# A four-layer transformer stack on one core: the experts' down projection with routed activations stationary

## The chip, the core and the metric

One core of one Trainium2 chip runs the whole program. The metric is the device time of one execution in microseconds (us). Engines are named as the profile names them: PE (TensorE matmul; PEld its weight loads), DVE (VectorE), ACT (ScalarE), POOL (GpSimd), SP (SyncE, which issues DMAs).

## What is computed

32 sequences of 256 tokens with 128 features run through four sublayers, each with a residual and a layer norm:

```python
x = ln(x + linear_attention(x))          # stage a
x = ln(x + low_rank_expert_ffn(x))       # stage b
x = ln(x + causal_softmax_attention(x))  # stage c
x = ln(x + moe(x))                       # stages r (router), d (experts), e (last norm)
```

The change lies in the last one. 16 experts of 64 hidden units are computed for every token, weighted by a grouped top-4 router, and a shared expert of 128 units is added:

```python
g = silu(einsum('th,efh->tef', x, w1_e)); u = einsum('th,efh->tef', x, w3_e)
routed = einsum('tef,ehf,te->th', g * u, w2_e, combine)
out = routed + (silu(x @ w1_s.T) * (x @ w3_s.T)) @ w2_s.T
```

## The kernel before

The tokens are cut into 16 blocks of 512 (four tiles of 128 tokens). The kernel is a software pipeline whose order is written out by hand, engine by engine: `turn(i)` issues stage a of block i, stage b and the start of c of block i-1, the rest of c and the router r of block i-2, the experts d of block i-3, and the last norm e of block i-4. There are 20 turns: six written out (LEAD), a loop of five passes with two turns each, four written out to drain. Engines wait for one another by semaphores with a counter per step; each engine runs its own list in order.

The experts' 16 x 64 hidden units and the shared expert's 128 are nine chunks of 128 units (ALLCH = 9). For chunk c, PE's `d_hidden` makes the gate (bank GB) and the up product (bank UB), three products of 512 columns each (L351 to L353; weights are split into a high and a low part). ACT's `d_silu` (L738) makes silu of GB, DVE's `d_gu` (L1067) multiplies by UB, and DVE's `d_hid` (L1077) by the router's weights, which lie transposed in bank CB; chunk 8, the shared expert, needs no weights and goes straight to hid (L1070). hid has 128 units on the partitions and 512 tokens along the free axis, two buffers. Then PE's `d_down` (L548) multiplies by the down weights w2: w2 is the stationary operand (128 x 128), hid streams through with 512 columns, and nine such products add up in bank YB. So YB holds y transposed: features on the partitions, tokens along. ACT's `d_y` (L740, at the end of the turn) copies YB to SBUF as yT, and PE's `d_yT` (L558) transposes its four tiles back into YB in the next turn, between the scores of stage c (`c_scores`) and the v product of stage a (`a_vT_`). DVE's `d_res` (L1079) adds the residual x3 and takes the norm's statistics.

Other steps that the prediction names: `a_vT_` waits for x0T_lo, which POOL makes (L1196) from ACT's copies of the transposed input; `c_av` (L510 to L512) multiplies the attention's probabilities, copied by ACT (L709, probT), with the values; `b_up` (L466, L467) waits for ACT's copy downT (L690); L454, L483 and L523 are other products whose stationary operand is an activation tile of 128 tokens. The small step L360 is the transpose of four tiles. At the program's end only e of the last block remains.

Of the kernel before, what the change touches and what calls it, by code (L numbers as in the profile page):

```python
# [26 lines left out]
ACT = mybir.ActivationFunctionType  # L27
# [5 lines left out]
P = 128  # L33
SEQ = 256
TILES = 4
BLOCK = TILES * P
# [7 lines left out]
CHUNKS = EXPERTS * EF // P  # L44
# [3 lines left out]
ALLCH = CHUNKS + 1  # L48
# [58 lines left out]
def started(n):  # L107

    return not (isinstance(n, int) and n == 0)


def build(nc, x_dram, weight_dram, whole_dram, out_dram):
# [13 lines left out]
    with ExitStack() as ctx:  # L126
        def sb(name, shape, dt=F32):
            return ctx.enter_context(nc.sbuf_tensor(name, shape, dt))

        def sig(name, per=1):  # L130
            return Signal(ctx.enter_context(nc.semaphore(name)), per)
# [3 lines left out]
        GB, UB, CB, YB = bank[0:4]  # L135
# [7 lines left out]
        whole = sb("whole", [P, N_CONST])  # L143
# [21 lines left out]
        def const(name, parts=P):  # L165
            a, b = CONST_COLS[name]
            return whole[0:parts, a:b]

        ident = const("ident")
# [99 lines left out]
        silu = sb("silu", [P, 2, BLOCK])  # L269
        gu = sb("gu", [P, 2, BLOCK])  # L270
        hid = sb("hid", [P, 2, BLOCK])
        yT = sb("yT", [P, BLOCK])


        w_in, k_in, late_in, x_st = sig("w_in"), sig("k_in"), sig("late_in"), sig("x_st", 16)
# [24 lines left out]
                                                        sig("a_exp", 4), sig("a_pT", 2), sig("v_rinv"))  # L300
        R_MASKED, R_TOP = 13, 17
        p_gate, a_ez, v_r, p_cT = sig("p_gate"), sig("a_ez"), sig("v_r", 29), sig("p_cT")
        p_G, p_U, p_w2, p_yT = sig("p_G", ALLCH), sig("p_U", ALLCH), sig("p_w2", ALLCH), sig("p_yT")
        a_silu, v_gu, v_hid, a_y = sig("a_silu", ALLCH), sig("v_gu", ALLCH), sig("v_hid", CHUNKS), sig("a_y")

        block = ctx.enter_context(nc.Block())

# [38 lines left out]
        def _(pe):  # L346
            mm = nc.tensor.matmul
# [7 lines left out]
            def tile(ap, t):  # L355
                return ap[:, t * P:(t + 1) * P]

            def transpose_tiles(out, src, eye, parts=P):
                for t in range(TILES):
                    last = nc.tensor.transpose(out[0:parts, t * P:(t + 1) * P], src(t), eye)  # L360
                return last
# [186 lines left out]
            def d_down(n, c):  # L548
                if c < CHUNKS:
                    pe.wait_ge(v_hid.sem, v_hid.at(n, c + 1))  # L550
                else:
                    pe.wait_ge(v_gu.sem, v_gu.at(n))
                if c == 0 and started(n):
                    pe.wait_ge(v_res[3].sem, v_res[3].at(n - 1))
                a = CONST_COLS["w2"][0] + c * P
                mm(YB[:], whole[:, a:a + P], hid[:, c % 2], start=c == 0, stop=c == CHUNKS).then_inc(p_w2.sem, 1)  # L556

            def d_yT(n):  # L558
                pe.wait_ge(a_y.sem, a_y.at(n))
                transpose_tiles(YB, lambda t: tile(yT, t), ident).then_inc(p_yT.sem, 1)  # L560

            def turn(i, odd, load=None):
                a, b, c, d, e = live(i), live(i - 1), live(i - 2), live(i - 3), live(i - 4)
                if a: a_xT_(i, odd, load)
                if d: d_hidden(i - 3, 1 - odd, 0)
                if d: d_cT(i - 3)
                if c: c_scores(i - 2)
                if e: d_yT(i - 4)
                if a: a_vT_(i)
                if d: d_hidden(i - 3, 1 - odd, 1)  # L570
                if c: c_pT(i - 2)
                if a: a_qk(i)
                if c: c_av(i - 2)
                if b: b_xT(i - 1)
                if a: a_g_(i)
                if d: d_down(i - 3, 0)
                if b: b_small(i - 1)
                if a: a_v_(i)
                if d: d_hidden(i - 3, 1 - odd, 2)
                if a: a_kv(i)  # L580
                if a: a_qT_(i)
                if d: d_hidden(i - 3, 1 - odd, 3)
                if d: d_down(i - 3, 1)
                if d: d_hidden(i - 3, 1 - odd, 4)
                if a: a_num_(i)
                if d: d_down(i - 3, 2)
                if c: r_xT(i - 2, odd)
                if d: d_down(i - 3, 3)
                if d: d_hidden(i - 3, 1 - odd, 5)
                if c: r_gate(i - 2)  # L590
                if b: b_dnT(i - 1)
                if d: d_down(i - 3, 4)
                if b: b_up(i - 1)
                if d: d_hidden(i - 3, 1 - odd, 6)
                if d: d_down(i - 3, 5)
                if a: a_aT(i)
                if d: d_hidden(i - 3, 1 - odd, 7)
                if d: d_down(i - 3, 6)
                if d: d_hidden(i - 3, 1 - odd, 8)
                if b: c_xT(i - 1)  # L600
                if a: a_out(i)
                if d: d_down(i - 3, 7)
                if b: c_project(i - 1)
                if d: d_down(i - 3, 8)
                if b: c_value(i - 1)
# [11 lines left out]
        def _(act):  # L617
            fn = nc.scalar.activation
# [118 lines left out]
                    act.wait_ge(v_gu.sem, v_gu.at(n, max(c - 1, 0)))  # L737
                fn(silu[:, c % 2], GB[:], ACT.Silu).then_inc(a_silu.sem, 1)  # L738

            def d_y(n):  # L740
                act.wait_ge(p_w2.sem, p_w2.at(n))
                fn(yT[:], YB[:], ACT.Copy).then_inc(a_y.sem, 1)

            def turn(i, odd):
                a, b, c, d, e = live(i), live(i - 1), live(i - 2), live(i - 3), live(i - 4)
                if d: d_silu(i - 3, 0)
                if a: x0_hi(i)
                if second(i): split_late()
                if c: c_exp(i - 2)
                if a: a_vT_(i)  # L750
                if c: c_pT(i - 2)
                if d: d_silu(i - 3, 1)
                if b: copy_xT(i - 1, 1, B0)
                if b: b_small(i - 1)
                if a: a_g_(i)
                if a: a_v_(i)
                if a: a_tap0(i)
                if d: d_silu(i - 3, 2)
                if a: a_qT_(i)
                if d: d_silu(i - 3, 3)  # L760
                if b: b_exp(i - 1)
                if c: c_norm(i - 2, odd)
                if d: d_silu(i - 3, 4)
                if c: r_hi(i - 2, odd)
                if d: d_silu(i - 3, 5)
                if c: r_exp(i - 2)
                if b: b_dnT(i - 1)
                if d: d_silu(i - 3, 6)
                if e: e_norm(i - 4)
                if d: d_silu(i - 3, 7)  # L770
                if b: b_layer_norm(i - 1)
                if d: d_silu(i - 3, 8)
                if b: copy_xT(i - 1, 2, B0)
                if b: c_qkv(i - 1)
                if d: d_y(i - 3)

            for i in range(LEAD):
                turn(i, i % 2)
# [8 lines left out]
        def _(dve):  # L787
# [18 lines left out]
            a, b = WEIGHT_COLS["logit"]  # L806
# [4 lines left out]
            a, b = WEIGHT_COLS["base"]  # L811
# [267 lines left out]
            def d_res(n, odd):  # L1079
                if started(n):  # L1080
                    dve.wait_ge(a_x4.sem, a_x4.at(n - 1))
                dve.wait_ge(p_yT.sem, p_yT.at(n))
                tt(res[3][:], x3[odd][:], tiles(YB[:]), ALU.add).then_inc(v_res[3].sem, 1)
                norm_stats(3, n)

# [217 lines left out]
```

## Time and profile before

| | us |
|---|---|
| median of 3 runs (lowest, highest) | 725.48 (723.78, 726.61) |
| span of the profiled execution | 722.4 |
| PE busy (weight loads PEld) | 659.3 (508.6) |
| DVE, ACT, POOL busy | 587.1, 486.4, 309.0 |

The profile gives no time of its own for the profiled execution beside its span from the first to the last instruction; the runs' median lies 3.1 us above it. Busy times are unions of instructions that overlap. A matmul's recorded length includes its way through the array and is modelled, so for a stream of products the step from one start to the next is the better measure. An f32 product shows as two records with a weight load each. "idle before" in brackets is the time in which the engine did nothing, and what ended it; "issue" means that nothing which the profile shows was waited for.

### The profile page before, as it was taken

The page shows a single profiled execution, that of the slowest core. Times are in us where ns is not written, and L with a number is a line of the kernel's source. Part 1 is how long each engine was busy: PE and PEld are TensorE (multiplying, and loading weights), DVE is VectorE, ACT ScalarE, POOL GpSimd, SP SyncE. Part 2 cuts the span into 40 slices and gives each one's busy share as a digit, 9 for nine tenths or more (in the row PEclk, how much of TensorE's full clock was granted, in tenths as well). Part 3 has the DMA queues.
Part 4 walks back from the last instruction along what each step waited for, and adds up shares of the span by engine and source line. Part 5 has one row for each costly group of instructions (what it writes and reads, how often), then busy time and mean ns, then how long its engine had stood idle before and what let it go on. Part 6 is the DMA issues. An engine that isn't in the chain of part 4 may idle for free.

```text
span 722.4 us, 13085 instructions
## 1 busy us (share of the span) xinstructions
PE 659.3 (91%) x3654; PEld 508.6 (70%) x3654; DVE 587.1 (81%) x1873; ACT 486.4 (67%) x978; POOL 309.0 (43%) x793
## 2 busy tenths in 40 slices
PE   3466679999999999999999999999999999999994
PEld 2354557787878777777878787777868787767652
DVE  1566778989898898889898898889897998877672
ACT  2243548587786878686877877686877868676623
POOL 1234443445453535536454535436454535340311
PEclk9787979999999999999999999999999999999997
DMA  6000000000000010101000000101000000000001
GB/s 226 12 4 15 1 16 0 16 1 16 15 15 15 1 30 2 31 0 29 0 15 16 5 25 0 30 0 29 0 21 9 15 0 0 15 1 15 16 0 30
DMA packets 18678, 12.51 MB, mean 17 GB/s; under 512 B 704, under 2 KB 18240, under 8 KB 18368
## 3 DMA queue, kind: packets, MB, share of 16 engines
q1 hardware_dynamic: 18624, 11.95, 5.5%
q8 instruction: 15, 0.25, 0.2%
q14 instruction: 39, 0.32, 0.1%
HBM read 7.75 MB, written 4.19 MB: 17 GB/s over the span
## 4 chain that ended last, share of the span: by engine, by line
PE 68%; DVE 14%; ACT 7%; issue 6%; POOL 3%; DMA 1%; DVEq 0%; ACTq 0%; SPq 0%; POOLq 0%
PE bank L556 13%; PE bank L351 8%; PE bank L353 8%; PE bank L352 8%; PE bank L360 8%; PE bank L439 2%; PE bank L466 2%; PE bank L411 2%; PE bank L454 2%; DVE conv L954 2%; DVE gu L1067 1%; PE bank L477 1%; PE bank L510 1%; PE bank L478 1%; PE bank L523 1%
## 5 line engine op out<-in xcount | busy, mean ns | idle before, releaser
L556 PE MATMUL bank<-hid,whole 128*128 128x512 f32 x288 | 147.2, 593 | 0.8 <-DVE hid L1070 0.8
L351 PE MATMUL bank<-x3T_hi,w_hi 128*128 128x512 f32 x288 | 138.2, 480 | 1.8 <-DVE gu L1067 1.4
L738 ACT ACTIVATE silu<-bank 128x512 f32<-128x512 f32 x144 | 86.4, 600 | 65.0 <-PE bank L353 61.9
L1067 DVE TENSOR_TENSOR gu<-silu,bank 128x512 f32<-128x512 f32 x128 | 86.7, 677 | 41.1 <-ACT silu L738 18.5
L353 PE MATMUL bank<-x3T_hi,w_lo 128*128 128x512 f32 x288 | 113.5, 394 | 0.0
L352 PE MATMUL bank<-x3T_lo,w_hi 128*128 128x512 f32 x288 | 112.7, 391 | 0.0
L1171 POOL TENSOR_TENSOR moment<-stats 128x4 f32<-128x4 f32 x192 | 44.8, 266 | 150.1 <-DVE stats L881 134.3
L1077 DVE TENSOR_TENSOR hid<-gu,bank 128x512 f32<-128x512 f32 x128 | 87.2, 681 | 1.8 <-PE bank L556 0.8
L351 PEld LDWEIGHTS bank<-x3T_hi,w_hi 128*128 128x128 f32 x288 | 54.2, 188 | 31.0 <-ACT silu L738 9.9
L1157 POOL TENSOR_TENSOR qk<-rope_c,rope_s 128x512 f32<-128x512 f32 x32 | 40.6, 1280 | 82.6 <-DVE rope_s L843 82.6
L1171 POOL TENSOR_TENSOR rstd<-moment,whole 128x4 f32<-128x4 f32 x64 | 64.7, 1011 | 5.0
L352 PEld LDWEIGHTS bank<-x3T_lo,w_hi 128*128 128x128 f32 x288 | 54.5, 189 | 16.3 <-issue 10.0
L353 PEld LDWEIGHTS bank<-x3T_hi,w_lo 128*128 128x128 f32 x288 | 54.0, 188 | 12.4
L556 PEld LDWEIGHTS bank<-hid,whole 128*128 128x128 f32 x288 | 49.7, 189 | 15.3 <-issue 7.2
L1201 POOL TENSOR_TENSOR x3T_lo<-x3T,x3T_hi 128x512 fp32r<-128x512 f32 x16 | 22.0, 1375 | 87.9 <-ACT x3T_hi L728 87.9
L738 ACT ACT_TABLE_LOAD x45 | 57.7, 1283 | 0.8
L954 DVE SCALAR_TENSOR_TENSOR conv<-vT,whole,conv 128x512 f32<-128x512 f32 x64 | 54.4, 850 | 0.8
L881 DVE BATCH_NORM_STATS2 stats<-res 128x6 f32<-128x128 f32 x192 | 41.9, 281 | 1.6
L1171 POOL TENSOR_TENSOR moment<-moment,whole 128x4 f32<-128x4 f32 x192 | 35.6, 202 | 5.0
L644 ACT ACTIVATE x<-bank,shift,rstd 128x128 f32<-128x128 f32 x64 | 24.1, 457 | 19.1 <-POOL shift L1171 19.1
L360 PEld LDWEIGHTS bank<-whole,x 128*128 128x128 f32 x192 | 23.7, 144 | 18.3 <-ACT x L644 7.9
L360 PE MATMUL bank<-whole,x 128*128 128x128 f32 x192 | 30.0, 280 | 7.1 <-ACT x L644 6.8
(196 smaller groups left out, 1635.7 us busy)
## 6 DMA issues: line engine op xcount, KB each, us to landing
x_in<-x SPq DMA_DIRECT2D x16, 256.0 KB, 2.9
out<-x SPq DMA_DIRECT2D x16, 256.0 KB, 2.3
whole<-w_whole SPq DMA_DIRECT2D x1, 1198.5 KB, 5.7
w_raw<-w SPq DMA_DIRECT2D x1, 1152.0 KB
w_raw<-w SPq DMA_DIRECT2D x1, 546.0 KB, 7.0
whole<-w_whole SPq DMA_DIRECT2D x16, 32.0 KB
whole<-w_whole SPq DMA_DIRECT2D x1, 64.0 KB
```

The lines of the kernel that those rows point to most:

```text
L351: mm(out, wh, mh, start=True, stop=False)
L352: mm(out, wh, ml, start=False, stop=False)
L353: return mm(out, wl, mh, start=False, stop=True)
L360: last = nc.tensor.transpose(out[0:parts, t * P:(t + 1) * P], src(t), eye)
L556: mm(YB[:], whole[:, a:a + P], hid[:, c % 2], start=c == 0, stop=c == CHUNKS).then_inc(p_w2.sem, 1)
L738: fn(silu[:, c % 2], GB[:], ACT.Silu).then_inc(a_silu.sem, 1)
L881: nc.vector.bn_stats(stats[k][:, t, :], res[k][:, t, :]).then_inc(v_st[k].sem, 1)
L954: stt(conv[:], vT[:, :, j:j + SEQ], taps[:, j:j + 1], conv[:], ALU.mult, ALU.add).then_inc(v_conv.sem, 1)
L1067: tt(gu[:, c % 2], silu[:, c % 2], UB[:], ALU.mult).then_inc(v_gu.sem, 1)
L1077: tt(hid[:, c % 2], gu[:, c % 2], CB[:], ALU.mult).then_inc(v_hid.sem, 1)
L1157: tt(qk[:, 2 * h:2 * h + 2, :].rearrange("p t d -> p (t d)"), rope_c[:, h], rope_s[:, h], ALU.add).then_inc(g_qk.sem, 1)
L1171: tt(out, in0, in1, op).then_inc(g_ln[k].sem, 1)
```

## The change

The operands of the down projection change places. For each chunk, each tile of 128 tokens of hid becomes the stationary operand, and w2's 128 columns stream through it: four products of 128 columns instead of one of 512. Each writes its own quarter of YB, so YB now holds y itself, tokens on the partitions, after nine chunks. The copy `d_y` on ACT, the transposes `d_yT` on PE, the buffer yT and their semaphores are gone; `d_res` on DVE waits for the last down product. Chunk 0's first product alone carries the start flag of the bank, the last product of chunk 8 the stop flag.

```diff
-                mm(YB[:], whole[:, a:a + P], hid[:, c % 2], start=c == 0, stop=c == CHUNKS).then_inc(p_w2.sem, 1)
-
-            def d_yT(n):
-                pe.wait_ge(a_y.sem, a_y.at(n))
-                transpose_tiles(YB, lambda t: tile(yT, t), ident).then_inc(p_yT.sem, 1)
+
+                for t in range(TILES):
+                    last = mm(tile(YB, t), hid[:, c % 2, t * P:(t + 1) * P], whole[:, a:a + P], start=c == 0 and t == 0,
+                              stop=c == CHUNKS and t == TILES - 1, skip_group_check=True)
+                last.then_inc(p_w2.sem, 1)
...
-                if e: d_yT(i - 4)
...
-            def d_y(n):
-                act.wait_ge(p_w2.sem, p_w2.at(n))
-                fn(yT[:], YB[:], ACT.Copy).then_inc(a_y.sem, 1)
...
-                if d: d_y(i - 3)
...
             def d_res(n, odd):
                 if started(n):
                     dve.wait_ge(a_x4.sem, a_x4.at(n - 1))
-                dve.wait_ge(p_yT.sem, p_yT.at(n))
+                dve.wait_ge(p_w2.sem, p_w2.at(n))
```

PE's list at the end of the loop's second turn, before. Banks are PSUM banks, `whole` holds the constants and w2, `x2T` is stage c's input; "x3" is three more of the same.

```order
L439 MATMUL bank<-whole,oT 128x128 [waits g_oT]
L439 MATMUL bank<-whole,oT 128x128 x3
L556 MATMUL bank<-hid,whole 128x512 [waits v_hid]
L477 MATMUL bank<-x2T,w_raw 128x512 [waits a_x2T]
L478 MATMUL bank<-x2T,w_raw 128x512
L552 REGISTER_ALU
L556 MATMUL bank<-hid,whole 128x512 [waits v_gu]
L483 MATMUL bank<-w_raw,x2T 128x128 [waits a_cq]
L483 MATMUL bank<-w_raw,x2T 128x128 x3
L609 COMPARE_AND_BRANCH
```

The same place after (line numbers move by one or two).

```order
L438 MATMUL bank<-whole,oT 128x128 [waits g_oT]
L438 MATMUL bank<-whole,oT 128x128 x3
L557 MATMUL bank<-whole,hid 128x128 [waits v_hid]
L557 MATMUL bank<-whole,hid 128x128 x3
L476 MATMUL bank<-x2T,w_raw 128x512 [waits a_x2T]
L477 MATMUL bank<-x2T,w_raw 128x512
L551 REGISTER_ALU
L557 MATMUL bank<-whole,hid 128x128 [waits v_gu]
L557 MATMUL bank<-whole,hid 128x128 x3
L482 MATMUL bank<-w_raw,x2T 128x128 [waits a_cq]
L482 MATMUL bank<-w_raw,x2T 128x128 x3
L607 COMPARE_AND_BRANCH
```

Nothing moves; each down product is four, and the first of them carries the wait. At the start of the loop's first turn PE's list before reads, from the last scores of stage c on (`x0T_hi` and `x0T_lo` are the two parts of stage a's transposed input, `x3T` those of the experts'):

```order
L497 MATMUL bank<-causal_b,ident_b 128x128
L498 MATMUL bank<-ckT,cqT 128x128
L360 MATMUL bank<-whole,yT 128x128 [waits a_y]
L360 MATMUL bank<-whole,yT 128x128 x3
L385 REGISTER_ALU
L351 MATMUL bank<-x0T_hi,w_hi 128x512 [waits v_res0,g_x0l]
L352 MATMUL bank<-x0T_lo,w_hi 128x512
L353 MATMUL bank<-x0T_hi,w_lo 128x512
```

And after:

```order
L496 MATMUL bank<-causal_b,ident_b 128x128
L497 MATMUL bank<-ckT,cqT 128x128
L384 REGISTER_ALU
L350 MATMUL bank<-x0T_hi,w_hi 128x512 [waits v_res0,g_x0l]
L351 MATMUL bank<-x0T_lo,w_hi 128x512
L352 MATMUL bank<-x0T_hi,w_lo 128x512
```

The two rows on yT are gone and what stood behind them follows at once. On DVE, `d_res` in the loop's first turn before:

```order
L886 TENSOR_SCALAR x<-res,mean,rstd 128x128 x3
L1081 ISA
L1083 TENSOR_TENSOR res<-x_0,bank 128x512 [waits p_yT,a_x4]
L881 BN_STATS stats<-res 128x6 [waits v_res3]
L881 BN_STATS stats<-res 128x6 x3
```

And after:

```order
L879 TENSOR_SCALAR x<-res,mean,rstd 128x128 x3
L1074 ISA
L1075 ISA [waits a_x4]
L1076 TENSOR_TENSOR res<-x_0,bank 128x512 [waits p_w2]
L874 BN_STATS stats<-res 128x6 [waits v_res3]
L874 BN_STATS stats<-res 128x6 x3
```

The add waits for the down product, and its wait for a_x4 has become a row of its own. The lists of POOL and SP are the same.

## Rows read from the trace of the kernel before

**Rows 1.** The page: busy time of each engine, and the granted clock by slices.
```profile
PE 659.3 (91%) x3654; PEld 508.6 (70%) x3654; DVE 587.1 (81%) x1873; ACT 486.4 (67%) x978; POOL 309.0 (43%) x793
...
PEclk9787979999999999999999999999999999999997
```

**Rows 2.** Timeline of PE at a turn's end: start, length, engine, line, what, [idle before].
```profile
421.01 1.02 PE L556 MATMUL bank<-hid,whole 128*128 128x512 f32 x2
421.87 1.05 PE L483 MATMUL bank<-w_raw,x2T 128*128 128x128 f32 x8
422.76 0.60 PE L360 MATMUL bank<-whole,x_in 128*128 128x128 f32 x4
```

**Rows 3.** Timeline of ACT, POOL and PE at the start of the next turn.
```profile
424.09 0.60 ACT L738 ACTIVATE silu<-bank 128x512 f32<-128x512 f32 x1 [1.42 <-PE bank L353]
...
425.80 1.28 POOL L1196 TENSOR_TENSOR x0T_lo<-x0T,x0T_hi 128x512 fp32r<-128x512 f32 x1 [2.25 <-ACT x0T L650]
...
426.79 0.60 PE L360 MATMUL bank<-whole,yT 128*128 128x128 f32 x4
427.15 0.49 PE L351 MATMUL bank<-x0T_hi,w_hi 128*128 128x512 f32 x1
...
430.51 0.85 ACT L709 ACTIVATE probT<-bank 128x384 f32<-128x384 f32 x2
...
431.42 0.49 PE L510 MATMUL bank<-cv,probT 128*128 128x128 f32 x2
```

**Rows 4.** Timeline of PE and DVE around the loop's jump back at 380 to 386 us.
```profile
351.12 0.38 PE L510 MATMUL bank<-cv,probT 128*128 128x128 f32 x1
...
358.13 0.69 DVE L1067 TENSOR_TENSOR gu<-silu,bank 128x512 f32<-128x512 f32 x1 [1.26 <-ACT silu L738]
...
381.37 1.05 PE L483 MATMUL bank<-w_raw,x2T 128*128 128x128 f32 x8
382.26 0.60 PE L360 MATMUL bank<-whole,x_in 128*128 128x128 f32 x4
...
385.93 0.69 DVE L1067 TENSOR_TENSOR gu<-silu,bank 128x512 f32<-128x512 f32 x1 [1.79 <-issue]
...
391.62 0.49 PE L510 MATMUL bank<-cv,probT 128*128 128x128 f32 x2 [0.47 <-ACT probT L709]
391.94 0.39 PE L511 MATMUL bank<-cv,probT 128*128 128x128 f32 x2
```

**Rows 5.** Timeline around chunk 4's down product: PE and ACT.
```profile
407.19 0.96 PE L523 MATMUL bank<-w_raw,x3T 128*128 128x16 f32 x8
407.99 0.62 PE L360 MATMUL bank<-whole,down_x 128*96 128x128 f32 x4
408.45 1.02 PE L556 MATMUL bank<-hid,whole 128*128 128x512 f32 x2
...
408.70 0.58 ACT L690 ACTIVATE downT<-bank 96x512 fp32r<-96x512 f32 x1
...
409.34 0.49 PE L466 MATMUL bank<-w_raw,x1T 128*128 128x128 f32 x2
```

**Rows 6.** Timeline of PE: two forms of product before a hidden product.
```profile
622.49 1.05 PE L483 MATMUL bank<-w_raw,x2T 128*128 128x128 f32 x8
...
623.62 0.39 PE L352 MATMUL bank<-x3T_lo,w_hi 128*128 128x512 f32 x1
...
637.29 1.02 PE L556 MATMUL bank<-hid,whole 128*128 128x512 f32 x2
...
638.38 0.40 PE L352 MATMUL bank<-x3T_lo,w_hi 128*128 128x512 f32 x1
```

**Rows 7.** Timeline of the last drained turns: the transposes, and the chain at the end.
```profile
691.64 0.60 PE L360 MATMUL bank<-whole,yT 128*128 128x128 f32 x4
...
711.76 0.60 ACT L742 ACTIVATE yT<-bank 128x512 f32<-128x512 f32 x1 [2.04 <-PE bank L556]
...
713.17 0.69 DVE L1083 TENSOR_TENSOR res<-x,bank 128x512 f32<-128x512 f32 x1 [2.63 <-PE bank L360]
```

More of the change, by code:

```diff
@@ L271, in build @@
         hid = sb("hid", [P, 2, BLOCK])
-        yT = sb("yT", [P, BLOCK])
         w_in, k_in, late_in, x_st = sig("w_in"), sig("k_in"), sig("late_in"), sig("x_st", 16)
@@ L302, in build @@
         p_gate, a_ez, v_r, p_cT = sig("p_gate"), sig("a_ez"), sig("v_r", 29), sig("p_cT")
-        p_G, p_U, p_w2, p_yT = sig("p_G", ALLCH), sig("p_U", ALLCH), sig("p_w2", ALLCH), sig("p_yT")
-        a_silu, v_gu, v_hid, a_y = sig("a_silu", ALLCH), sig("v_gu", ALLCH), sig("v_hid", CHUNKS), sig("a_y")
+        p_G, p_U, p_w2 = sig("p_G", ALLCH), sig("p_U", ALLCH), sig("p_w2", ALLCH)
+        a_silu, v_gu, v_hid = sig("a_silu", ALLCH), sig("v_gu", ALLCH), sig("v_hid", CHUNKS)
         block = ctx.enter_context(nc.Block())
```

## The prediction

> **What bounds the kernel now.** I read the page first. PE is busy 91% of the span and PEclk is 9 in all but the first slices, so TensorE runs at its full clock level in the middle [rows 1]. In 40 us of timeline from the middle, PE's records follow each other with hardly a gap. The reader is to see three things there.
>
> First, what a down product costs. Its two records are recorded 1.02 us long, but ends are modelled, so I use the step from one group's start to the next: 421.01 to 421.87, 0.86 us [rows 2].
>
> Second, the short stretch at the start of a turn, from silu of chunk 0 to the attention product L510. PE is *not* alone on the path there. POOL's x0T_lo starts at 425.80 and takes 1.28, to 427.08; PE's next product that needs it (L351 on x0T_hi) starts at 427.15, right after the four yT transposes (426.79 to 427.15) [rows 3]. No row of ACT shows idle time from 424.09 (silu) to 431.36, the end of the second probT copy (430.51 + 0.85), and L510 starts at 431.42, with no idle time of PE noted before it [rows 3]. So PE, POOL and ACT arrive together, within a few hundredths of a microsecond.
>
> Third, the turn that follows the loop's jump back. DVE's gu comes 1.79 us late there with "issue" as reason, the row maxima and so ACT's exponentials are late, and PE stands idle for 0.47 us before L510 [rows 4]. Back from that gu, DVE has no other gap to 358.13, where it waited for ACT's silu of chunk 2 of the turn before [rows 4]. L510 to L510 is 431.42 - 391.62 = 39.80 us without the jump and 391.62 - 351.12 = 40.50 with it [rows 3, 4]. There are 4 jumps (5 passes of two turns).
>
> **What it removes.** Per block: four transposes on PE, one ACT copy of 0.60 us, and two hand-overs between engines. The ACT copy is worth nothing inside: ACT is idle 1.42 us right behind it, until PE has produced chunk 0's first product [rows 3]. The transposes (0.36 us from start to start) are worth nothing inside either: without them PE is done with c_scores at 426.79, but x0T_lo is there only at 427.08, as before. PE then waits about 0.3 us instead of transposing, and further on probT would hold it anyway. Value taken in a whole turn: 0; its bounds are 0 and 0.36. Only at the very end, where nothing else runs, the chain shows: ACT's copy starts at 711.76 and DVE's residual add at 713.17 [rows 7]; the add now waits for the product itself, so the end comes 713.17 - 711.76 = 1.41 us earlier. In turn 18 (a drained one) PE has just waited for comb, and the transposes at 691.64 lie between that and hidden chunk 1 [rows 7]. There up to 0.36 goes; since the next products wait for DVE's gu too, I take 0.26.
>
> **What it adds.** 144 chunks each have four products of 128 columns (eight records, eight weight loads) for one of 512 columns (two and two). The trace has the same form: L483, four f32 products of 128 columns, each with a new activation tile stationary. It takes 421.87 to 422.76, 0.89 us [rows 2]. That is 111 ns a record, against 0.43 us for 512 columns. Are the loads hidden? L523 has only 16 columns, so its eight loads set its pace: 407.19 to 407.99, 0.80 us or 100 ns a load [rows 5]. 100 is under 111, so yes. The Trainium skill, "TensorE: Matmul & The Clock Gate", section "Back-to-back issue gap", gives N/2.4 + 2.5 ns per matmul; by it six more records would cost an estimated 15 ns a chunk, and the sum below would come out near 0 and not at +1.6; the rows show more than that per short f32 record, and I go by the rows.
>
> What follows counts too. Three of a turn's nine chunks stand before a hidden product, whose first load has little to hide behind. From the down product to L352's start the old form takes 637.29 to 638.38, 1.09 us; the short form, L483 before the same product, 622.49 to 623.62, 1.13 [rows 6]. So +0.04 there, +0.03 elsewhere: I take **35 ns a chunk**. Its lower bound is 0 (the columns streamed are the same, so a gain is out); the upper one follows under the rivals.
>
> Where does it count? Chunk 4 is hidden: behind it L466 starts at 409.34, and ACT's downT ends at 408.70 + 0.58 = 409.28; the product itself, from 408.45, would be through at 408.45 + 0.86 = 409.31 [rows 5]. PE waits there by 0.03 already, so chunk 4 may grow by that at no cost. The other eight lie between L510 and the next silu of chunk 0, where PE is full: 8 x 0.035 = **+0.28 us a turn**. In the four turns with a jump, DVE holds the end of the interval, and its chain hangs on hidden chunk 2; of the eight only chunk 0 comes before that, so +0.035, and the other 0.25 vanish in the 0.47 us that PE stood waiting.
>
> DVE's add waits for p_w2 and not p_yT: it was never late for its transposes but at the end, and p_w2 comes sooner; nothing behind it on DVE changes. In one of the loop's two turns a wait becomes an instruction of its own on DVE (the order shows it): it comes after the row maxima, off the chain above, and costs nothing. POOL and SP have the same rows. PE's products and loads grow from 3654 to 3654 + 144 x 6 - 64 = 4454 each.
>
> **The sum.** The blocks end at L510 of turns 4 to 16: 9 intervals without a jump x 0.28 = +2.52; 4 with it x 0.035 = +0.14; the three drained turns +0.3 (some 16 chunks that count x 0.035 = 0.56, less 0.26); the end -1.41 + 0.035 = -1.38. With d for the price of a chunk that is 72d + 4d + 16d - 0.26 + d - 1.41 = 93d - 1.67. Together **+1.6 us**: the span goes from 722.4 to 724.0. The span lies 3.1 us below the median of the runs, 725.48; what lies around it stays, so 727.1.
>
> **The rivals.**
> A, the forecast above: 727.1.
> B, the transposes' time is real gain. If the tie at L351 and L510 is looser than I read it (another order of arrival in other turns), the nine intervals lose 0.36 each: 1.6 - 3.2 = -1.6, so 723.9; in the jump turns too, 722.4. Against it: POOL's row and PE's start fit to 0.07, and ACT has no gap.
> C, the short products are dearer. When the stream is broken, the first product takes 391.62 to 391.94, 0.32, where one of L483's takes 0.89 / 4 = 0.22 [rows 2, 4]. If each chunk pays half of that break, 0.05, on top of 0.035, then 93 x 0.085 - 1.67 = +6.2: 731.7. With the whole break it is 93 x 0.135 - 1.67 = +10.9, and the jump turns' slack is used up, so some 737; that is the upper bound. It decides from 0.057 us a chunk on, where +3.6 is reached. Against it: L483 begins with a load of an activation tile too, and its 0.89 contains it.
> D, PE's loop body grows by 200 products and loads in all (100 a turn), and PE too starts to lose time at the jump, as DVE does with 1.79 us. Now it loses none: from L483 to the x_in transposes it is 0.89 at a jump (381.37 to 382.26) and 0.89 without [rows 2, 4]. If it lost DVE's 1.79 less the 0.47 that PE stands there anyway, 4 x 1.3 = +5.3 comes on top: 732.4. The Trainium skill, "Runtime: NRT & Kernel Launch", section "Instruction fetch mechanics", says that a taken branch whose target has left the engine's instruction window forces a fetch; by that rule a longer body could lose its start, and DVE's row agrees with it; that PE's body stays inside is shown by no row for the longer one.
> E, the change doesn't do what it says: the order shows the four products and no yT row, so this is out.
>
> **How the numbers follow.** A 0.68, B 0.12, C 0.10, D 0.06, anything else 0.04. The runs lie within 0.25% of their median, and about 0.5% (3.6 us) is what a measurement can tell from no change. Faster means under 721.9: part of B and of the rest, 0.05. Slower means over 729.1: C and D but for their mild ends, and a part of the rest, 0.15. Same: 0.80. The range is B's 723 to 730.5, which leaves out most of C and D and half of the rest, together under 0.2.
>
> **What would show it.** In the profile after: chunk to next group 0.89 instead of 0.86; PE's wait for POOL's x0T_lo, hidden before, now in nearly every turn with about 0.3 us; L510 to L510 near 40.08 without a jump and 40.53 with one; no gap on ACT before probT; the end 1.4 us shorter from the last product on. A gap of PE behind the jump speaks for D, groups over 0.95 for C, and intervals under 39.8 for B. If ACT's chain from silu of chunk 0 to probT gets shorter than 431.36 - 424.09 = 7.27 us, my main step is wrong.

## The result, and the profile of the changed kernel

The changed kernel takes 726.19 us (median), the kernel before 725.07 us: a ratio of 1.0015, 95% interval 1.0009 to 1.0021. That is 1.1 us more, 0.7 to 1.5 by the interval. The forecast was +1.6 us, 727.1 us in all, with a chance of 0.80 on "same".

The page of the changed kernel: busy time, granted clock, and the shares of the chain that ended last.

```profile
PE 661.8 (91%) x4454; PEld 585.2 (81%) x4454; DVE 587.0 (81%) x1873; ACT 475.6 (66%) x962; POOL 308.2 (43%) x793
...
PEclk9778969999999999999999999999999999999997
...
PE 64%; DVE 13%; ACT 9%; issue 7%; POOL 5%; DMA 1%; DVEq 0%; ACTq 0%; SPq 0%; POOLq 0%
```

PE has its 4454 products and as many loads, and it is busy only 2.5 us longer than in [rows 1]; loads are busy 77 us longer and hardly show. The clock is the same in the long middle.

Timeline of the changed kernel, PE at a turn's end, the lines that answer to [rows 2]: one chunk's short products, then the 128-column products after it.

```profile
423.83 1.05 PE L557 MATMUL bank<-whole,hid 128*128 128x128 f32 x8
424.72 1.06 PE L482 MATMUL bank<-w_raw,x2T 128*128 128x128 f32 x8
425.61 0.60 PE L359 MATMUL bank<-whole,x_in 128*128 128x128 f32 x4
```

The chunk takes 424.72 - 423.83 = 0.89 us where it took 0.86.

Timeline of ACT, POOL and PE at the start of the next turn (answers to [rows 3]), and PE behind a jump of the loop (answers to [rows 4]).

```profile
426.95 0.60 ACT L736 ACTIVATE silu<-bank 128x512 f32<-128x512 f32 x1 [2.23 <-PE bank L352]
...
428.66 1.27 POOL L1189 TENSOR_TENSOR x0T_lo<-x0T,x0T_hi 128x512 fp32r<-128x512 f32 x1 [2.49 <-ACT x0T L648]
...
429.38 0.44 PE L497 MATMUL bank<-ckT,cqT 128*128 128x128 f32 x2
429.99 0.51 PE L350 MATMUL bank<-x0T_hi,w_hi 128*128 128x512 f32 x1 [0.17 <-POOL x0T_lo L1189]
...
433.36 0.85 ACT L707 ACTIVATE probT<-bank 128x384 f32<-128x384 f32 x2
...
434.27 0.48 PE L509 MATMUL bank<-cv,probT 128*128 128x128 f32 x2
```

```profile
394.20 0.49 PE L509 MATMUL bank<-cv,probT 128*128 128x128 f32 x2 [0.40 <-ACT probT L707]
```

The four transposes of yT are gone from between the scores (L497) and v's transposed product (L350), and in their place PE waits for POOL's x0T_lo, which ends at 428.66 + 1.27 = 429.93. The row says 0.17 of idle time, but ends of products are modelled; the whole step from L497 to L350 is 0.61 us, and a kernel shown below does it in 0.20 us when nothing is waited for. The product by probT (L509 now, L510 before) comes 434.27 - 394.20 = 40.07 us after the one before it; it was 39.80 in [rows 3, 4].

The waits of PE on POOL and ACT at these two places: in all us, times, longest.

```profile
PE bank L350 <- POOL x0T_lo L1189: 11.1, 16, 5.0
...
PE bank L509 <- ACT probT L707: 3.3, 7, 0.8
```

The wait for x0T_lo stands there 16 times, 12 of them in the twelve whole turns from turn 4 on; before it was 3 times, all ahead of 112 us.

The end, which answers to [rows 7]: the last chunks' products and DVE's last residual add.

```profile
712.87 2.16 PE L557 MATMUL bank<-whole,hid 128*128 128x128 f32 x16
...
715.14 0.69 DVE L1076 TENSOR_TENSOR res<-x,bank 128x512 f32<-128x512 f32 x1 [1.32 <-PE bank L557]
```

The add waits for the product itself.

The table divides the profiled executions by the product by probT, which every block has once. "Plain" is the mean of the eight intervals (ending at turns 4 to 7, 9, 11, 13, 15) without a jump of the loop, "jump" the mean of the four with one (turns 8, 10, 12, 14), which differ by up to 0.3 us within one profile where PE waits for probT; "16" and "17" are the intervals that end at these drained turns, "end" the time from turn 17's product to the end of the span. The experiments of the next section stand in it too. All in us; the medians of before that were taken beside the experiments are 725.15 (the two halves, the cut in 4, x0_hi first), 724.70 (the cut in 2, and the two with both) and 725.42 (probT first).

| kernel | plain | jump | 16 | 17 | end | median | ratio to before, interval |
|---|---|---|---|---|---|---|---|
| before, two profiles | 39.80, 39.79 | 40.58, 40.54 | 38.03, 38.03 | 35.16, 35.17 | 56.96, 56.90 | 725.07 | |
| after, two profiles | 40.07, 40.08 | 40.61, 40.55 | 37.96, 37.98 | 34.87, 34.87 | 55.94, 55.96 | 726.19 | 1.0015 [1.0009, 1.0021] |
| before without transposes | 39.80 | 40.63 | 37.70 | 34.84 | 55.56 | 722.92 | 0.9974 [0.9963, 0.9986] |
| products alone | 40.08 | 40.54 | 38.33 | 35.19 | 57.33 | 728.04 | 1.0043 [1.0029, 1.0056] |
| before, product cut in 4 | 40.10 | 40.56 | 38.32 | 35.19 | 57.36 | 727.08 | 1.0038 [1.0024, 1.0051] |
| before, product cut in 2 | 39.84 | 40.50 | 38.08 | 35.17 | 56.96 | 725.30 | 1.0012 [1.0003, 1.0022] |
| after, x0_hi first | 39.95 | 40.65 | 38.00 | 34.86 | 55.94 | 725.43 | 1.0010 [1.0001, 1.0019] |
| after, probT first | 39.98 | 40.05 | 37.92 | 34.88 | 55.94 | 722.79 | 0.9962 [0.9948, 0.9976] |
| after, both | 39.58 | 39.63 | 37.88 | 34.88 | 55.91 | **717.43** | 0.9914 [0.9899, 0.9929] |
| before, probT first | 39.71 | 39.76 | 37.94 | 35.16 | 56.95 | 720.14 | 0.9929 [0.9916, 0.9942] |
| before, both | 39.69 | 39.69 | 37.92 | 35.17 | 56.92 | 720.04 | 0.9935 [0.9922, 0.9947] |

From before to after, with the means of the two profiles: 8 x 0.28 = +2.25 in the plain turns, +0.1 in the four with a jump, -0.06, -0.29 and -0.98 in the drain: together +1.0 us, against +1.1 by the medians. The two spans shown, 722.4 and 724.3, lie 1.9 us apart: another 1.0 us stands before turn 3, where no step of the change works.

### The profile page after: what moved, and what is told of

Same layout as the page of the kernel before. It is cut to its first block, busy times and chain, and to the rows that moved or that the text cites. A ratio compares the mean times of both kernels' runs of the same rounds, so it can differ in the third digit from the quotient of the medians.

```text
span 724.3 us, 14669 instructions
## 1 busy us (share of the span) xinstructions
PE 661.8 (91%) x4454; PEld 585.2 (81%) x4454; DVE 587.0 (81%) x1873; ACT 475.6 (66%) x962; POOL 308.2 (43%) x793
## 4 chain that ended last, share of the span: by engine, by line
PE 64%; DVE 13%; ACT 9%; issue 7%; POOL 5%; DMA 1%; DVEq 0%; ACTq 0%; SPq 0%; POOLq 0%
PE bank L557 13%; PE bank L350 8%; PE bank L352 8%; PE bank L351 8%; PE bank L359 7%; POOL x0T_lo L1189 2%; PE bank L465 2%; PE bank L438 2%; PE bank L410 2%; PE bank L453 2%; PE bank L476 2%; DVE conv L947 2%; DVE gu L1060 2%; PE bank L482 2%; PE bank L477 1%
## 5 line engine op out<-in xcount | busy, mean ns | idle before, releaser
L557 PEld LDWEIGHTS bank<-whole,hid 128*128 128x128 f32 x1152 | 146.1, 192 | 14.0 <-issue 7.2
L557 PE MATMUL bank<-whole,hid 128*128 128x128 f32 x1152 | 152.1, 275 | 0.8 <-DVE hid L1063 0.6
L350 PE MATMUL bank<-x3T_hi,w_hi 128*128 128x512 f32 x288 | 124.3, 432 | 1.7 <-DVE gu L1060 1.4
L351 PE MATMUL bank<-x3T_lo,w_hi 128*128 128x512 f32 x288 | 112.7, 391 | 0.0
L350 PEld LDWEIGHTS bank<-x3T_hi,w_hi 128*128 128x128 f32 x288 | 54.5, 189 | 11.8 <-DVE gu L1060 3.4
L351 PEld LDWEIGHTS bank<-x3T_lo,w_hi 128*128 128x128 f32 x288 | 54.7, 190 | 6.3
L1189 POOL TENSOR_TENSOR x0T_lo<-x0T,x0T_hi 128x512 fp32r<-128x512 f32 x16 | 20.3, 1267 | 37.1 <-ACT x0T L648 37.1
```

The lines of the kernel that those rows point to most:

```text
L350: mm(out, wh, mh, start=True, stop=False)
L351: mm(out, wh, ml, start=False, stop=False)
L557: last = mm(tile(YB, t), hid[:, c % 2, t * P:(t + 1) * P], whole[:, a:a + P], start=c == 0 and t == 0, stop=c == CHUNKS and t == TILES - 1 ...
```

## The experiments

The theory (T) is the prediction's: in a whole turn the transposes' time is worth nothing, because x0T_lo and then probT hold TensorE anyway; the short products cost 35 ns a chunk; only the drain gains. The main rivals say that the transposes' time is real in every turn (B), and that the price has another source than the short records.

**The change in its two halves.** One kernel takes only the transposes and the copy away, the other takes only the new products.

```diff
-                if e: d_yT(i - 4)
...
-                if d: d_y(i - 3)
...
-                dve.wait_ge(p_yT.sem, p_yT.at(n))
+                dve.wait_ge(p_w2.sem, p_w2.at(n))
```

> The kernel before without ACT's copy yT and without TensorE's four transposes of it; the products stay as they were, one of 512 columns a chunk. Left out: y is added to x3 as it stands in the bank, untransposed. Theory T (the transposes' 0.36 us is hidden in a whole turn, because x0T_lo and the chain of ScalarE to probT hold TensorE anyway): the intervals from one vT-after-probT transpose to the next stay at 39.80 us in the turns without a loop jump and at 40.5 to 40.6 in those with one; about 0.3 us of waiting for x0T_lo appears ahead of v's transposes; only the drain and the end get shorter, by 0.36 + 0.4 + 1.4 us: about 2.2 us below before, ratio 0.997. Rival B (the transposes' time is real in every turn): 39.44 us in the turns without a jump, so 8 x 0.36 = 2.9 us more: about 5.1 us below before, ratio 0.993; 6.5 below (0.991) if the turns with a jump gain as well.

```diff
-                mm(YB[:], whole[:, a:a + P], hid[:, c % 2], start=c == 0, stop=c == CHUNKS).then_inc(p_w2.sem, 1)
+                for t in range(TILES):
+                    last = mm(tile(YB, t), hid[:, c % 2, t * P:(t + 1) * P], whole[:, a:a + P], ...)
+                last.then_inc(p_w2.sem, 1)
```

> Only the products are changed, to four of 128 columns a chunk with the routed activations stationary; ACT's copy yT and the four transposes stay, so that y is transposed once too often within each tile of 128 tokens (that part of the result is another one than the reference's). Theory T (the products alone cost 0.27 us a turn without a jump, the transposes are worth nothing there): 40.07 us in these turns, as in the changed kernel; 40.6 with a jump; no gain in the drain or at the end, about 0.3 us lost in each drained turn instead: 2.2 + 0.1 + 0.6 = about 2.9 us above before, ratio 1.004. Rival B (the change's products cost 0.27 + 0.36 us a turn, and the transposes' 0.36 is given back): 40.43 us in the turns without a jump, about 5.8 us above before, ratio 1.008.

Without the transposes: 722.92 us, 2.2 below before. The plain turns stay at 39.80 us to the hundredth, and the whole gain lies in the drain (-0.33, -0.32, -1.40 from the first profile of before: 2.05). PE's waits and the same place of a turn in this kernel:

```profile
PE bank L351 <- POOL x0T_lo L1194: 11.2, 16, 5.1
```

```profile
428.89 0.44 PE L498 MATMUL bank<-ckT,cqT 128*128 128x128 f32 x2
429.51 0.50 PE L351 MATMUL bank<-x0T_hi,w_hi 128*128 128x512 f32 x1 [0.18 <-POOL x0T_lo L1194]
```

The same 16 waits as in the changed kernel, and the same step from the scores to v's product, 0.62 us (there 0.61), which the transposes filled before. Rival B would have had 39.44 us. The kernel with the products alone takes 728.04 us, 2.9 above before, with 40.08 us a plain turn and no wait for x0T_lo after 112 us. T had 2.2 below for the one and 2.9 above for the other. The two halves add up to within 0.05 us: +0.28 and 0.00 make the +0.28 of a plain turn, +0.30 - 0.33 and +0.03 - 0.32 are near the -0.06 and -0.29 of turns 16 and 17, +0.37 - 1.40 near the -0.98 of the end.

**What the price of the products follows.** The operands stay as before (w2 stationary), and the product of 512 columns is cut in four of 128 or in two of 256.

```diff
-                mm(YB[:], whole[:, a:a + P], hid[:, c % 2], start=c == 0, stop=c == CHUNKS).then_inc(p_w2.sem, 1)
+                for t in range(TILES):
+                    last = mm(tile(YB, t), whole[:, a:a + P], hid[:, c % 2, t * P:(t + 1) * P], ...)
+                last.then_inc(p_w2.sem, 1)
```

> The kernel before with w2 stationary as it was, but each product of 512 columns cut into four of 128 columns with a load of the same w2 chunk ahead of each. Theory T (the price of the changed products is that of four short products and four loads for one, whichever operand is stationary): 1152 + records of 128 columns where the change has them, 0.89 us a chunk, 40.07 us in the turns without a jump, about 2.9 us above before, ratio 1.004, the same as the kernel with the changed products alone. Rival O (the price comes from the operands' change of places: hid, written by VectorE a moment ago, must now be loaded before a product can start): 0.86 us a chunk, 39.80 us a turn, ratio 1.000.

The cut in two has `range(2)` with columns `h * 2 * P:(h + 1) * 2 * P`.

> The kernel before with each product of 512 columns cut into two of 256 columns, the same w2 chunk loaded ahead of both; the result is the reference's. It measures what the price of the change's products follows. Theory N (the number of records and loads: six more of each cost 35 ns a chunk when one product is cut in four, so two more cost about 12 ns): 0.868 us a chunk, 39.80 + 8 x 0.012 = 39.89 us in a turn without a jump, about 0.9 us above before, ratio 1.0012. Theory W (the narrowness: a load of 128 columns takes about as long as a record of 128 columns and sometimes shows beside it, never beside one of 256): 0.857 us a chunk, 39.80 us a turn, ratio 1.000.

Timeline of PE in the kernel cut in four, one chunk at a turn's end, and what follows it:

```profile
422.64 1.05 PE L557 MATMUL bank<-hid,whole 128*128 128x128 f32 x8
423.53 1.06 PE L483 MATMUL bank<-w_raw,x2T 128*128 128x128 f32 x8
```

The groups by line, PE: records, busy us, mean ns of one. The first fence is of the kernel before, the second of the one cut in two, the third of the one cut in four.

```profile
L556 PE MATMUL bank<-hid,whole 128*128 128x512 f32 x288 | 147.2, 593 | 0.8 <-DVE hid L1070 0.8
```

```profile
L558 PE MATMUL bank<-hid,whole 128*128 128x256 f32 x576 | 147.9, 379 | 0.8 <-DVE hid L1074 0.8
```

```profile
L557 PE MATMUL bank<-hid,whole 128*128 128x128 f32 x1152 | 151.9, 275 | 0.6 <-DVE hid L1073 0.6
```

The cut in four costs what the change's products cost: 423.53 - 422.64 = 0.89 us a chunk, 40.10 us a plain turn, and the same drain. (Its 727.08 us is 1.9 above before where T had 2.9; against the products alone, its profile differs only ahead of turn 3, by 1.3 us, a stretch that the last experiment is about.) So the new places of the operands are free, and rival O is out: the load of a freshly written hid tile doesn't show. The cut in two costs little: from start to start a chunk (the median of those that stand before no hidden product) takes 0.858, 0.864 and 0.891 us for one, two and four products (0.892 in the changed kernel). That is 6 ns for two more records and 33 for six more, so neither theory's number is met: it is under N's 12 ns, and over W's 0 in the plain turns (39.84).

The Trainium skill, "TensorE: Matmul & The Clock Gate", section "Back-to-back issue gap", gives N/2.4 + 2.5 ns as the isolated gap of a single matmul. For a stream of loads and products the same section gives 81 ns a matmul at 128 columns and 131 ns at 512; the records here take neither time, and the rows decide. The Trainium skill, "FP8 and Floating Point Precision", section "TensorE Precision Notes", says that true FP32 takes four passes through the array. The trace has two records for each f32 product, 111 ns apart at 128 columns, 216 at 256 and 429 at 512, which is near two passes each by the formula of the isolated gap (an estimate of 112, 218 and 432). Counted by passes, the cut in four adds twelve times 2.5 = 30 ns, near the 33 measured, and the cut in two 10, against 6. The prediction had counted the formula by records and got 15.

**Which wait stands behind which.** In the changed kernel ACT's order is altered: x0_hi, from which x0T_lo is made, ahead of the first silu.

```diff
-                if d: d_silu(i - 3, 0)
                 if a: x0_hi(i)
+                if d: d_silu(i - 3, 0)
```

> The changed kernel with one swap in ScalarE's order: the copy x0_hi(i), which POOL's x0T_lo waits for, stands ahead of the silu of chunk 0 instead of behind it. The result is the reference's. Theory T (with the transposes gone, TensorE waits 0.28 us for x0T_lo in every turn without a jump): x0T_lo comes earlier by ScalarE's time for the silu, the wait goes, and the turns without a jump fall from 40.07 to between 39.71 (39.80 + 0.27 - 0.36) and 39.80 us: 2.2 to 2.9 us below the changed kernel, so 1.1 to 1.8 us below before, ratio 0.998. Rival R (ScalarE's own chain to probT, 7.27 us from the silu of chunk 0 in this order, is as tight as x0T_lo): the wait moves to the v transposes behind probT and the turns stay at 40.0 to 40.1 us, ratio to before 1.0015 as for the changed kernel; slower than that if the later silu makes the hidden product wait.

725.43 us, a ratio of 1.0010 to before where the changed kernel had 1.0015. The plain turns fall by 0.13 us to 39.95 and no further. The waits and the timeline of this kernel:

```profile
PE bank L350 <- POOL x0T_lo L1189: 8.5, 3, 5.0
...
PE bank L509 <- ACT probT L707: 6.6, 16, 0.8
```

```profile
428.89 0.44 PE L497 MATMUL bank<-ckT,cqT 128*128 128x128 f32 x2
429.09 0.47 PE L350 MATMUL bank<-x0T_hi,w_hi 128*128 128x512 f32 x1
...
433.65 0.49 PE L509 MATMUL bank<-cv,probT 128*128 128x128 f32 x2 [0.17 <-ACT probT L707]
```

The waits for x0T_lo are gone from the whole turns, and 9 more waits for probT have come. Here is the step of 0.20 us without a wait; so the wait that took the transposes' place is 0.61 - 0.20 = 0.41 us long, and the transposes with what they break cost PE 0.44 (0.468 us from the scores' last record to v's first with them, 0.031 here). Rival R was right on the mechanism, and the size lies between the two: T had not followed ACT's chain to probT, though the prediction had ("further on probT would hold it anyway").

**Both waits away.** ACT copies probT ahead of neg_mean and v_cent, which PE only needs several microseconds later.

```diff
                 if a: a_vT_(i)
                 if c: c_pT(i - 2)
+                if a: a_cent_(i)
```

where a_cent_ is the second half of a_vT_ (neg_mean and the two v_cent). Four kernels have this: the changed one and the one before, each with and without x0_hi first.

> The changed kernel with both of ScalarE's orders changed: x0_hi(i) ahead of the silu of chunk 0, as in the run before, and the two copies probT ahead of neg_mean and the two v_cent, which only transposes several microseconds later read. The result is the reference's. Theory T (each wait that the removed transposes laid bare, x0T_lo first and probT second, is off TensorE's path now, and nothing third is as tight): the turns without a loop jump fall to what TensorE's instructions take by themselves, 40.08 us of the kernel with the changed products alone less 0.36 us of transposes = 39.72 us, and the gap ahead of the product by probT from 0.45 to about 0.12 us; 8 x 0.35 = 2.8 us below the changed kernel, 1.7 us below before, ratio 0.9977. Rival Q (a third wait, by the pattern of the two runs so far: the silu of chunk 1 or v's transposes come 0.85 us later in this order and hold TensorE or VectorE): the turns stay near 39.94 us, ratio 1.000 to 1.001.

> The kernel before (one product of 512 columns a chunk, ACT's copy yT, four transposes) with the same two changes of ScalarE's order as in the run beside it. The result is the reference's. Theory T (in the kernel before TensorE is already full in a turn without a jump: it waits neither for x0T_lo nor, beyond 0.02 us, for probT): no change, 39.78 to 39.80 us a turn, ratio 0.999 to 1.000. Rival B' (ScalarE's chain holds part of the turn of the kernel before as well, so that the order of ScalarE and not the transposes is what a gain comes from): turns below 39.6 us, ratio below 0.998.

> The changed kernel with only the second change of ScalarE's order: the two copies probT ahead of neg_mean and v_cent; the silu of chunk 0 stays ahead of x0_hi. The result is the reference's. Theory T (two separate waits: x0T_lo's follows the hidden product of chunk 0 at a fixed distance of silu, two copies and POOL, and stays; probT's goes): the wait of 0.28 us for x0T_lo stays in the turns without a loop jump, these fall only by the 0.11 us by which the six products by probT got shorter in the kernels with both changes (1.34 for 1.44 us, a load that no longer stands behind probT), to 39.96 us; the turns with a jump lose their wait of 0.56 us for probT too and fall from 40.6 to about 40.0 us: 8 x 0.11 + 4 x 0.65 = 3.5 us below the changed kernel, 2.4 us below before, ratio 0.9967. Rival P (the order of probT does everything, the silu's place nothing): 39.6 us in all turns, ratio 0.9915 as with both.

> The kernel before with only the two copies probT put ahead of neg_mean and v_cent. The result is the reference's. Theory T (here x0T_lo holds nothing, since the transposes of yT stand ahead of v's; probT held 0.11 us in every turn and 0.6 to 0.7 us more in those with a jump): 39.69 us in all turns, as with both changes, about 4.5 us below before, ratio 0.9938. Rival X (the earlier x0T_lo has a part in it): the turns without a jump stay over 39.75 us, those with one over 39.9 us, ratio over 0.995.

With both, the changed kernel takes 717.43 us, and the one before 720.04. T had 1.7 us below before for the one and no change for the other; they are 7.3 and 4.7 below. T missed both. For the kernel before, rival B' was nearer: the ratio is below its 0.998, though a plain turn is 39.69 us and not below 39.6; most of the gain lies in the turns with a jump. PE's rows in the one before with both, a product by probT behind a jump and the next without one:

```profile
389.81 0.38 PE L510 MATMUL bank<-cv,probT 128*128 128x128 f32 x2
...
429.50 0.38 PE L510 MATMUL bank<-cv,probT 128*128 128x128 f32 x2
430.83 0.38 PE L360 MATMUL bank<-whole,x 128*128 128x128 f32 x2
```

Two things were overlooked. A plain turn of the kernel before was not free of probT: its first product by probT loads only when ACT's copy has ended, and from there the six products take 432.86 - 431.42 = 1.44 us to the next group, here 430.83 - 429.50 = 1.33. That 0.11 us a turn is the price of a tie that no idle time shows. The row of the kernel before that ends this step, after the last of [rows 3], and the load of its first product:

```profile
432.86 0.60 PE L360 MATMUL bank<-whole,x 128*128 128x128 f32 x4
```

```profile
431.41 0.30 PEld L510 LDWEIGHTS bank<-cv,probT 128*128 128x128 f32 x2
```

The same load in the kernel before with both:

```profile
429.38 0.31 PEld L510 LDWEIGHTS bank<-cv,probT 128*128 128x128 f32 x2
```

The first load starts right behind ACT's copy (431.36) and with its product (431.42) in the one, and 0.12 us ahead of its product (429.50) in the other.

And the 0.8 us that a jump cost were not DVE's to decide, but came to PE through ACT's chain. The timeline of the kernel before with only probT first, DVE and ACT and PE behind a jump:

```profile
383.93 0.69 DVE L1070 TENSOR_TENSOR gu<-silu,bank 128x512 f32<-128x512 f32 x1 [1.90 <-issue]
...
385.18 0.37 ACT L705 ACTIVATE prob<-bank,neg_max 128x128 f32<-128x128 f32 x1 [0.82 <-DVE neg_max L1013]
...
387.49 0.90 ACT L711 ACTIVATE probT<-bank 128x384 f32<-128x384 f32 x2
388.23 0.25 ACT L672 ACTIVATE neg_mean<-v_sum 128x2 f32<-128x2 f32 x1
388.51 0.91 ACT L675 ACTIVATE v_cent<-vT,neg_mean 128x256 f32<-128x256 f32 x2
...
388.86 0.38 PE L510 MATMUL bank<-cv,probT 128*128 128x128 f32 x2
```

DVE still loses 1.90 us at the jump, ACT's exponentials still wait 0.82 us for it, but probT is copied by 387.49 + 0.90 = 388.39 and PE doesn't wait: 39.76 us with a jump, 39.71 without. So the change of ACT's order is worth 4.7 to 5.3 us to the kernel before. The two runs with probT first alone were planned from this reading, and came out by it (rival P is out). For the kernel before: 39.69 us and ratio 0.9938 expected, 39.71 and 0.9929 measured, so that the earlier x0_hi adds little there: 0.02 us a plain turn and 0.07 a turn with a jump, which is 39.69 us with it (rival X is out); for the changed kernel: 39.96 us, about 40.0 with a jump and 0.9967 expected, 39.98, 40.05 and 0.9962 measured. There x0T_lo still holds the turn, as PE's rows of that kernel show:

```profile
428.85 0.50 PE L350 MATMUL bank<-x0T_hi,w_hi 128*128 128x512 f32 x1 [0.17 <-POOL x0T_lo L1192]
...
433.11 0.38 PE L509 MATMUL bank<-cv,probT 128*128 128x128 f32 x2
433.33 0.39 PE L510 MATMUL bank<-cv,probT 128*128 128x128 f32 x2
```

Either wait alone keeps the changed kernel at 39.95 to 39.98 us a plain turn; only without both does the transposes' time come out: 39.58 us. PE's rows of the changed kernel with both, behind a jump and at the next turn (427.50 - 387.89 = 39.61):

```profile
387.89 0.38 PE L509 MATMUL bank<-cv,probT 128*128 128x128 f32 x2
...
427.50 0.38 PE L509 MATMUL bank<-cv,probT 128*128 128x128 f32 x2
```

In the two kernels with both, PE has no wait in any of the twelve whole turns, and there the change is worth -0.11 us a plain turn. The transposes' -0.44 and the products' +0.28 would make -0.16; where the other 0.05 us are was not looked for. With its drain it makes the changed kernel 717.43 us against 720.04, 2.6 us faster: the same change that costs 1.1 us in the order that it was put into. The medians are of six and five runs, and these overlap (716.54 to 720.29 and 719.18 to 720.24); the intervals of the table, from turn 4 on, give 2.5 us.

**The profiles once more.** Both kernels were profiled a second time, unchanged.

> The kernel before once more, unchanged, to have a second profile of it: in the first one the interval between the products by probT of turns 2 and 3 is 36.99 us, in the changed kernel's 38.25 us, 1.0 us of the difference between the two profiled spans, though no step of the change works there. If this belongs to the execution (the granted clock's phase in the first 120 us) and not to the change, the second profile shows it at about 38.25 us as likely as at 37; if it belongs to the change's absence, 37.0 us again. The turns without a jump stay at 39.80 us either way.

> The changed kernel once more, unchanged, for a second profile: the second profile of the kernel before had 38.28 us between turns 2 and 3 where the first had 36.99 us, so this stretch belongs to the execution; here anything from 37 to 38.3 us can come out of it. The turns without a jump are 40.07 us again, with about 0.28 us of waiting for x0T_lo in each, and those with a jump 40.5 to 40.7 us.

The lead-in's interval between turns 2 and 3 is 38.28 us in both, after 36.99 and 38.25 in the first profiles. The product by probT of turn 3 in the first and the second profile of before:

```profile
111.52 0.38 PE L510 MATMUL bank<-cv,probT 128*128 128x128 f32 x1
```

```profile
112.86 0.34 PE L510 MATMUL bank<-cv,probT 128*128 128x128 f32 x1
```

So the 1.0 us before turn 3 belongs to the execution and not to the change. The second spans, 723.5 and 724.6, are 1.2 us apart, as the medians are. What makes this stretch long or short was not pursued.

## Why the prediction was right, point by point

**The transposes are worth nothing in a whole turn: right, and shown** by the kernel without them (39.80 us for 39.80). Its mechanism was right too: x0T_lo first, probT behind it. The size of the wait was not: about 0.3 us was read from 426.79 to 427.08 [rows 3], and it is 0.41. The step L360 to L351, 0.36 us, misses what the transposes add before their own first record.

**35 ns a chunk: right.** 33 to 34 ns were measured, in either place of the operands. +0.28 us a turn came out as +0.28 (0.273 and 0.290 by the two pairs of profiles). That chunk 4 costs nothing was not quite so: in the twelve whole turns it costs 0.01 on average. Chunk 3, with the hidden products behind it, costs about 0.02 in the turn compared (404.92 to 407.19 us before, 407.61 to 409.90 after), where 0.035 was taken.

**+0.035 in turns with a jump: right in number, wrong in part of its reason.** The mean moved by +0.02, but single turns with a jump differ by up to 0.3 us within one profile, so this number can't be told from 0. And "DVE holds the end of the interval" took ACT's order for given: with probT first, the same loss on DVE (1.90 us) costs 0.05 us.

**The sum: one interval mis-sized.** Turn 16 was counted as one more plain interval, +0.28; it measured -0.06. The block that makes x0T_lo no longer runs there, so nothing takes the transposes' place and their 0.33 us is real. The last drained turns and the end, +0.30 - 1.38 = -1.08, measured -1.27: the price of the last chunks is 0.40 (the kernel with the products alone) where 0.60 was taken, and the transposes and the copy give 0.32 + 1.40 = 1.72 where 0.26 + 1.41 were. Together these are 0.5 us, which is the difference between +1.6 and +1.1. The time of 727.1 us lies another 0.4 us too high because it starts from 725.48, the median of three runs, where twenty runs have 725.07.

**The rivals.** B needed the transposes' time to come back in every plain turn, 39.44 us without them; the kernel without them has 39.80, so B is out in this order of ACT, though most of that time does come back once both waits are gone. C is out: no chunk takes 0.95 us to the next group in a whole turn; the longest, chunk 4, takes 0.92 with its wait for downT. D is out: PE loses nothing at the jump, and the wait for probT behind it is no longer than before (0.40 for 0.47 us of idle time). The changed kernel's PE at a jump:

```profile
384.05 1.06 PE L482 MATMUL bank<-w_raw,x2T 128*128 128x128 f32 x8
384.94 0.60 PE L359 MATMUL bank<-whole,x_in 128*128 128x128 f32 x4
```

From the last products of a turn to the first transposes of the next it is 0.89 us here, as it is without a jump (424.72 to 425.61). DVE, in contrast, is 1.75 to 2.10 us late behind every jump of every profile. The Trainium skill, "Runtime: NRT & Kernel Launch", section "Instruction fetch mechanics", says that a taken branch whose target lies outside the current instruction window first forces a fetch of it. DVE's rows agree with that, but no run here shows the fetch itself.

**The signs named in advance.** A chunk takes the 0.89 us that was named. PE waits for x0T_lo in 16 places. A plain turn has 40.07 us for the 40.08 forecast, a turn with a jump 40.61 for 40.53, and ACT has no gap ahead of probT. The end gets 1.4 us shorter by the copy and the transposes (56.96 to 55.56 without them), of which the last products take 0.4 back. ACT's chain from silu to the end of probT takes 434.21 - 426.95 = 7.26 us for 7.27.

## What to carry to other kernels

Instructions taken off the busiest engine are worth what the next arrival at that place leaves: list who else arrives within the time that is taken out (here x0T_lo within 0.1 us and probT right behind), and move those first; the same edit then went from +1.1 to -2.6 us. A copy on which the busy engine waits belongs ahead of those that are read later: moving two copies ahead of three instructions of the same engine was worth 5.3 us to the kernel before, where the change moved 1.1. And a tie that shows no idle time can still cost: here 0.11 us a turn, by a weight load that was not made ahead.

No run touched one part of ACT's chain to probT: a row ACT_TABLE_LOAD of 1.28 us (425.68 to 426.96 in the kernel before) stands in its 7.27 us, ahead of the first exponential.

## What the runs showed of the hardware that was not expected

A product by probT whose stationary operand PE had to wait for takes 0.32 us to the next one's start (391.62 to 391.94 [rows 4]), against 0.22 when the operand was there in time (433.11 to 433.33 in the changed kernel with probT first). Cutting an f32 product of 512 columns in four adds 33 to 34 ns, with either operand stationary, and cutting it in two adds 6; the weight load ahead of each record of 128 columns hides, as the records still follow each other by 111 ns. DVE loses 1.75 to 2.10 us at every jump of the loop in all the profiles, and whether the kernel loses anything by it depends here on ACT's order: in the kernel before, 0.8 us a jump with probT behind neg_mean and v_cent, 0.05 with probT ahead of them.
